# A two-layer mixture-of-experts and attention kernel: earlier index compaction, outputs on ScalarE, gathers issued ahead of scatters

## The chip, the cores and the metric

One core of a Trainium2 chip runs the whole program. The metric is the device time of one execution in microseconds. Before the change three runs gave 1326.40, 1332.17 and 1331.73 us, median 1331.73.

## The reference

For x of 4 batches, 1024 tokens and 128 features, all in float32:

```
x = x + 0.5 * ffn(layernorm(x))
x = x + attention(layernorm(x))     # 16 heads of 8, 3D rotary positions
x = x + 0.5 * ffn(layernorm(x))     # same weights
```

In ffn eight experts each choose the 256 tokens of a batch with the highest affinity (a softmax over experts), and

```
x_in = x[bidx, idx]                          # gather, 256 rows per batch and expert
h = silu(x_in @ w_gate.T) * (x_in @ w_up.T)  # 128 -> 512
x_e = h @ w_down.T                           # 512 -> 128
out = zeros.at[bidx, idx].add(gating * x_e)  # scatter-add
```

## The kernel before, in words

There are three stages: experts, attention, experts. Each expert stage works through 16 passes, 0 to 15 and 16 to 31: first the eight experts for batches 0 and 1, then the eight for batches 2 and 3. Pass `it` (function `expert` of each engine) handles 512 rows, 256 of each of two batches. All engines have an instruction order of their own, written out by hand, and meet only at semaphores, each of which is named `s_...`.

**The way of one expert j.** DVE (VectorE) builds a one-hot matrix of 128 x 256 for each of 16 token blocks (`onehots`, L1362, in quarters of four). TensorE multiplies it by a table with five columns for each token: two parts of the row number, three parts of the gating factor (`compact`, L1041, 32 small matmuls). DVE reads the result from PSUM (`pick`, L1369 to L1377): row numbers `idx`, factors `gain`. POOL (GpSimd) issues four indirect DMAs, 128 rows each, that gather the tokens (`gather`, L535). TensorE transposes them (`turn_tokens`, L1051), ScalarE copies them out of PSUM (L784). Then come the gate and up projections in four slices (`gate_up`, L1061 and L1062), silu on ScalarE (L793), the product on DVE (`hidden`, L1394), the down projection (`down`, L1072), scaling by `gain` out of PSUM (`outputs`, L1385, on DVE), and four indirect DMAs that add the rows in DRAM (`scatter`, L553).

**How the passes overlap.** In pass `it` TensorE computes gate and up of expert `it` in slices 0 to 3. Behind slice 1 it computes the down projection of expert `it - 1` and then compacts expert `it + 2`; behind slice 2 it transposes the tokens of expert `it + 1`. DVE calls `outputs(it - 1)` and then `pick(it + 2)` behind the second product. POOL calls `scatter(it - 1)` and then `gather(it + 2)`. SP loads the weights of expert j after the down projection of expert j - 2.

**Waits around the change.** A gather waits for its indices and for the transposes of expert j - 2. A scatter waits for its outputs and until the scatter before it, into the same rows' tensor, has landed. `pick(j)` writes buffer j % 4 and, at L1369 to L1371, waits until the scatter of expert j - 4, which reads its indices there, has landed:

```
                if j >= 4:
                    for b in batches(j - 4):
                        dve.wait_ge(s_scat[b], adds_before(j - 4) + 32)
```

`hidden(it, u)` waits for silu; `gate_up(it + 1, 0)` on TensorE waits for `hidden(it, 2)`. In front of slot tables (`all_onehots`) `expert_values` copies the slots and factors of one expert into `slotE` and `valsE`.

**What stands between.** The table of `tables()` puts other work at places (it, k), done by `between`: in passes 0 to 5 and 16 to 22 the search for the routing thresholds of the next half ("f": a scan of 1024 affinities on DVE, L1275, then a small matmul, ten rounds), in passes 10 to 15 the attention's projections ("s": a matmul into one bank of PSUM, which DVE or ScalarE must read before the next). For the attention each rotated projection is split into three bfloat16 parts: `high` and `middle` on ScalarE, `rest` (L580) and `lowest` (L584) on POOL. The factors of the next half are split in three by `gains` on POOL (L566 to L576). After scatter 6 and 7, and after 14 and 15, SP reloads X (`load_x`), of which DVE takes the moments in pass 9 and in the attention. SP then stores the parts and loads the groups for the attention (`store_parts`, `load`). The attention starts on TensorE when the outputs of expert 15 are written.

## Time and profile before

| | us |
|---|---|
| median of three runs | 1331.73 |
| profiled execution | 1333.52 |
| its span, first to last instruction | 1331.7 |
| DVE busy | 1044.5 |
| TensorE busy (matmul) | 1122.5 |
| ScalarE busy | 768.2 |
| POOL busy | 448.9 |
| mean granted TensorE clock | 0.944 of 2.4 GHz |

Busy times are sums over the whole span; the stages have different limits, so a share says little of a single one. In the profile a line such as L1072 is a line of the kernel, "x32" counts instructions merged in the row, and what stands behind "<-" is what ended the idle time in front of it. POOL's rows for indirect DMAs are the time of issuing them; the data lands later. Names of tiles are those of the memory: `xt`, `ye`, `sg` and `hid` all lie in `Pt`.

### The profile page before, as it was taken

What the parts mean: (1) busy time and instruction counts of PE and PEld (TensorE: products, weight loads), DVE (VectorE), ACT (ScalarE), POOL (GpSimd) and SP (SyncE); (2) the same over time, 40 slices, a digit from 0 to 9 for tenths busy, and PEclk for the clock granted to TensorE, in tenths of its full rate; (3) what the DMA queues carried; (4) which work ended last, traced back from release to release, by engine and by line L of the source; (5) the groups of instructions that cost most, each with busy time, mean ns of one, the idle gap of its engine ahead of it and who ended that gap; (6) DMA issues with size and microseconds to landing.
All of it is one profiled execution on the core that took longest, in us unless ns stands there. A gap on an engine that the chain in (4) does not pass through costs nothing.

```text
span 1331.7 us, 25142 instructions
## 1 busy us (share of the span) xinstructions
PE 1122.5 (84%) x9424; PEld 476.4 (36%) x9424; DVE 1044.5 (78%) x2182; ACT 768.2 (58%) x1433; POOL 448.9 (34%) x431
## 2 busy tenths in 40 slices
PE   3159898999487999999899998899978889889884
PEld 3126565666131222222222222122313256556553
DVE  3676966764986999999999999899896685975531
ACT  2043112532246999999789996889778843121120
POOL 3034777688256111100000000004000025777674
PEclk9999999999587999999999998999999988999887
DMA  8023446456612311112201131101220224444442
GB/s 264 6 56 68 82 86 141 82 128 139 174 43 80 87 31 38 43 43 52 63 17 31 41 82 48 40 8 41 73 57 4 56 58 95 100 87 85 104 89 20
DMA packets 92122, 94.54 MB, mean 71 GB/s; under 512 B 14464, under 2 KB 68992, under 8 KB 91968
## 3 DMA queue, kind: packets, MB, share of 16 engines
q1 hardware_dynamic: 69472, 76.13, 20.5%
q0 software_dynamic: 22528, 16.79, 9.6%
q8 instruction: 75, 1.23, 0.4%
q14 instruction: 47, 0.39, 0.1%
HBM read 63.12 MB, written 31.59 MB: 71 GB/s over the span
## 4 chain that ended last, share of the span: by engine, by line
DVE 50%; PE 25%; POOL 8%; issue 7%; ACT 5%; DMA 3%; DVEq 0%; POOLq 0%; ACTq 0%
DVE mx L1549 34%; PE pA L1072 4%; PE pS L1061 4%; DVE ge L1275 4%; POOL out_dram L553 3%; PE pO L1185 3%; PE pO L1062 2%; DMA xg<-zd,idx 2%; DVE onehot L1362 2%; POOL x L553 2%; ACT Pt L893 2%; DVE scr L1434 2%; PE pS L1206 2%; POOL xg L535 2%; PE pS L1062 1%
## 5 line engine op out<-in xcount | busy, mean ns | idle before, releaser
L1549 DVE TENSOR_REDUCE mx<-pA 128x2 f32<-128x1024 f32 x512 | 589.3, 1216 | 26.8 <-PE pA L1117 25.3
L893 ACT ACTIVATE Pt<-pS 128x512 f32<-128x512 f32 x1024 | 556.2, 596 | 75.7 <-PE pS L1206 70.3
L1185 PE MATMUL pO<-Pt,Vst 128*16 128x256 f32 x4096 | 327.9, 393 | 11.5 <-ACT U L884 11.5
L793 ACT ACTIVATE Pt<-pS 128x512 f32<-128x512 f32 x128 | 76.3, 597 | 245.6 <-PE pS L1061 245.4
L595 POOL TENSOR_TENSOR mparts<-mx,onesm 128x32 bf16<-128x32 f32 x16 | 4.0, 252 | 518.0 <-DVE mx L1554 511.3
L1117 PE MATMUL pA<-Kst,Qst 48*128 48x512 bf16 x704 | 144.3, 406 | 36.6 <-DVE mx L1549 34.8
L535 POOL DMA_INDIRECT xg<-zd,idx x128 | 125.7, 982 | 142.0 <-issue 73.1
L1061 PE MATMUL pS<-Pt,wg 128*128 128x512 f32 x256 | 147.6, 660 | 14.5 <-DVE Pt L1394 9.4
L1206 PE MATMUL pS<-Qst,Kst 51*128 51x512 bf16 x704 | 141.5, 398 | 10.7 <-ACT Pt L893 5.1
L1185 PEld LDWEIGHTS pO<-Pt,Vst 128*16 128x16 f32 x4096 | 68.3, 94 | 206.5 <-issue 116.7
L1072 PEld LDWEIGHTS pA<-wd,Pt 128*128 128x128 f32 x1024 | 120.9, 192 | 20.3 <-issue 15.0
L1072 PE MATMUL pA<-wd,Pt 128*128 128x128 f32 x1024 | 122.3, 276 | 2.2 <-DVE Pt L1394 2.2
L553 POOL DMA_INDIRECT x<-Pt,idx x64 | 101.0, 1578 | 58.2 <-issue 29.0
L1362 DVE TENSOR_SCALAR onehot<-slots,slotE 128x256 bf16<-128x256 bf16 x512 | 115.9, 305 | 1.4
L1206 PEld LDWEIGHTS pS<-Qst,Kst 51*128 51x128 bf16 x704 | 34.5, 93 | 166.4 <-ACT Pt L893 147.6
L1394 DVE TENSOR_TENSOR Pt<-Pt,pO 128x512 f32<-128x512 f32 x64 | 43.9, 686 | 62.3 <-PE pO L1062 47.0
L1385 DVE TENSOR_SCALAR Pt<-pA,gain 128x128 f32<-128x128 f32 x128 | 36.0, 344 | 60.2 <-PE pA L1072 56.1
L1062 PE MATMUL pO<-Pt,wu 128*128 128x512 f32 x128 | 71.1, 639 | 0.0
L1062 PE MATMUL pS<-Pt,wu 128*128 128x512 f32 x128 | 69.1, 623 | 0.0
L1117 PE MATMUL pA<-pair 48*128 48x512 bf16 x320 | 62.8, 388 | 5.8 <-DVE mx L1549 5.8
L1394 DVE TENSOR_TENSOR Pt<-Pt,pS 128x512 f32<-128x512 f32 x64 | 43.8, 685 | 29.5 <-ACT Pt L793 14.3
L784 ACT ACTIVATE Pt<-pA 128x512 f32<-128x512 f32 x32 | 19.1, 596 | 81.9 <-PE pA L1051 81.9
(170 smaller groups left out, 1140.0 us busy)
## 6 DMA issues: line engine op xcount, KB each, us to landing
wg<-w_gate_dram SPq DMA_DIRECT2D x32, 256.0 KB, 2.8
wu<-w_up_dram SPq DMA_DIRECT2D x32, 256.0 KB, 3.1
wd<-w_down_dram SPq DMA_DIRECT2D x32, 256.0 KB, 3.9
qk<-parts SPq DMA_DIRECT2D x64, 96.0 KB, 2.7
Kst<-qk SPq DMA_DIRECT2D x132, 32.0 KB
zd<-Z SPq DMA_DIRECT2D x8, 512.0 KB, 4.1
vp<-pair SPq DMA_DIRECT2D x4, 1024.0 KB, 5.3
Vst<-vp SPq DMA_DIRECT2D x16, 256.0 KB
```

Source lines behind the costliest of these rows:

```text
L535: pool.indirect_dma_start(xg[p][:, k, :], None, zd[j // E % 2], bass.IndirectOffsetOnAxis(idx[j % 4][:, k:k + 1], 0)).then_inc(s_gath[p], 16)
L553: pool.indirect_dma_start(acc, bass.IndirectOffsetOnAxis(rows[j % 4][:, k:k + 1], 0), ye[j % 2][:, k, :], None, compute_op=ALU.add).then_i ...
L893: S.activation(Pt[:, s % 4, j, r * 512:(r + 1) * 512], pS[:, bank_of(k, 4 * s + 2 * j + r), :], ACT.Exp, scale=SCALE).then_inc(s_exp, 1)
L1061: M.matmul(pG[u % 2], wg[p][:, u * P:(u + 1) * P], xt[:, p, :], start=True, stop=True).then_inc(s_gate, 1)
L1062: M.matmul(pU[u % 2], wu[p][:, u * P:(u + 1) * P], xt[:, p, :], start=True, stop=True).then_inc(s_up, 1)
L1072: last = M.matmul(pY[:, k * D:(k + 1) * D], hid[p][:, i, k * P:(k + 1) * P], wd[p][:, i, :], start=(i == 0), stop=(i == IC - 1))
L1117: last = M.matmul(pA[ring[q, a] % 2][:, r, :], Qst[k][64 * r:64 * r + 48, j, c * P:(c + 1) * P], Kst[k][64 * r:64 * r + 48, j, half * 512: ...
L1185: last = M.matmul(pO[32 * h:32 * h + 16, cols], Vst[k][:, s % 8, h, :], Pt[:, s % 4, h // 2, (h % 2) * 512 + 256 * a:(h % 2) * 512 + 256 * ...
L1206: last = M.matmul(pS[:, bank_of(k, n + r), :], Kst[k][64 * r:64 * r + ROWS, j, (s % 8) * P:(s % 8 + 1) * P], Qst[k][64 * r:64 * r + ROWS, ...
L1362: last = V.tensor_scalar(onehot[:, b, c, :], slots[:, :], slotE[:, c * HB + b:c * HB + b + 1], None, ALU.is_equal)
L1394: V.tensor_tensor(hid[it % 2][:, u, :], sg[:, u % 2, :], pU[u % 2], ALU.mult).then_inc(s_hid, 1)
L1549: V.reduce_max(mx2[:, k, 2 * j:2 * j + 2, c, half], pA[ring[q, a] % 2][:, :, :], AX.X).then_inc(s_Ar, 1)
```

## The change

TensorE compacts expert `it + 2` right behind gate and up slice 1, ahead of the down projection. DVE picks behind the second product, ahead of `between(it, 1)`; it sums the parts straight out of PSUM, with one conversion to integers behind it. `expert_values` goes: one-hots and compaction read `slotT` and `vals` in place. `outputs` runs on ScalarE, behind `between(it, 1)`, with the factor as the activation's scale. POOL issues `gather(it + 2)` ahead of `scatter(it - 1)`, except in pass 22. `rest` and `lowest` of tiles 0 and 1 run on DVE in passes 12 to 14; those of tiles 2 and 3 stay on POOL, behind `scatter(15)`, and ScalarE's `middle(2)` moves behind pass 15. On SP `load(0)`, `load(1)` and `store_values(1)` come ahead of the weights of expert 16, and `store_parts(2)` comes behind the reload of X.

```diff
@@ SP
+            load(0)
+            load(1)
+            store_values(1)
             load_weights(16)
-            load(0)
             load_weights(17)
-            store_parts(2)
-            store_values(1)
             for b in range(2, B):
                 sp.wait_ge(s_scat[b], 256)
                 load_x(b, x1_in)
+            store_parts(2)
             store_parts(3)
-            load(1)
@@ POOL
             for it in range(RUN):
-                if 13 <= it:
-                    lowest(it - 13)
-                if it in (12, 13):
-                    rest(it - 12)
+                if it + 2 < RUN:
+                    gather(it + 2)
                 if it:
                     scatter(it - 1)
-                if it + 2 < RUN:
-                    gather(it + 2)
                 if it == 2:
                     gains(1)
-                if it in (14, 15):
-                    rest(it - 12)
             scatter(RUN - 1)
+            rest(2)
+            rest(3)
+            lowest(2)
             lowest(3)
...
             for it in range(RUN, NIT):
+                if it + 2 < NIT and it != 22:
+                    gather(it + 2)
                 if it > RUN:
                     scatter(it - 1)
-                if it + 2 < NIT:
+                if it == 22:
                     gather(it + 2)
@@ ScalarE
+            def outputs(j):
+                act.wait_ge(s_down, j + 1)
+                act.wait_ge(s_idx, j + 1)
+                if j >= 2:
+                    for b in batches(j - 2):
+                        act.wait_ge(s_scat[b], adds_before(j - 2) + 32)
+                for k in range(HB * SH):
+                    last = S.activation(ye[j % 2][:, k, :], pY[:, k * D:(k + 1) * D], ACT.Copy, scale=gain[j % 4][:, k:k + 1])
+                last.then_inc(s_ye, 1)
...
                         between(it, 1)
+                        if it % RUN:
+                            outputs(it - 1)
                         between(it, 2)
@@ TensorE
                 gate_up(it, 1)
+                if it % RUN < RUN - 2 and it != 22:
+                    compact(it + 2)
                 if not first:
                     down(it - 1, (0, 1))
                 between(it, 1)
                 if not first:
                     down(it - 1, (2, 3))
-                if it % RUN < RUN - 2 and it != 22:
-                    compact(it + 2)
@@ DVE, pick
-                link(V.tensor_copy(picked[r][:, :, :], pI[:, 0:5 * HB * SH].rearrange("p (k f) -> p k f", f=5)))
-                V.tensor_tensor(idx[r][:, :], picked[r][:, :, 0], picked[r][:, :, 1], ALU.add).then_inc(s_idx, 1)
+                picked = pI[:, 0:5 * HB * SH].rearrange("p (k f) -> p k f", f=5)
+                V.reduce_sum(gain[r][:, :], picked[:, :, 2:5], AX.X)
+                V.reduce_sum(row[:, :], picked[:, :, 0:2], AX.X).then_inc(s_row, 1)
+                dve.wait_ge(s_row, j + 1)
+                V.tensor_copy(idx[r][:, :], row[:, :]).then_inc(s_idx, 1)
...
-                link(V.tensor_tensor(gsum[:, :], picked[r][:, :, 2], picked[r][:, :, 3], ALU.add))
-                link(V.tensor_tensor(gain[r][:, :], gsum[:, :], picked[r][:, :, 4], ALU.add))
@@ DVE, expert
                 hidden(it, 1)
-                between(it, 1)
-                if not first:
-                    outputs(it - 1)
                 if it + 2 < end and it != 22:
                     pick(it + 2)
-                    if quarters:
-                        expert_values(it + 3)
-                        onehots(0)
+                between(it, 1)
+                if it + 2 < end and it != 22 and quarters:
+                    onehots(it + 3, 0)
                 between(it, 2)
```

## Rows read from the trace of the kernel before

**Rows 1.** the page, busy time of each engine

```profile
PE 1122.5 (84%) x9424; PEld 476.4 (36%) x9424; DVE 1044.5 (78%) x2182; ACT 768.2 (58%) x1433; POOL 448.9 (34%) x431
```

**Rows 2.** the page, shares of the chain that ended last, by engine

```profile
DVE 50%; PE 25%; POOL 8%; issue 7%; ACT 5%; DMA 3%; DVEq 0%; POOLq 0%; ACTq 0%
```

**Rows 3.** windows, passes 3, 12, 25, 26: length, PE, PEld, DVE, ACT, POOL busy, clock, DMA

```profile
132.00:149.00 17.00, 13.28 (x90) 8.31 (x89) 16.30 (x59) 2.99 (x5) 13.96 (x15) 0.96 0.40 78
...
266.00:281.30 15.30, 15.30 (x100) 9.97 (x99) 10.51 (x34) 5.66 (x11) 12.54 (x10) 1.00 0.45 88
...
1211.30:1223.70 12.40, 12.40 (x85) 8.16 (x84) 7.87 (x31) 2.99 (x5) 7.61 (x7) 0.95 0.43 99
1223.70:1241.50 17.80, 14.11 (x86) 8.81 (x85) 7.95 (x31) 2.99 (x5) 14.45 (x11) 0.86 0.47 84
```

**Rows 4.** timeline of TensorE in pass 24; start us, us, what, idle before

```profile
1199.69 3.73 PE L1072 MATMUL pA<-wd,Pt 128*128 128x128 f32 x32
1203.27 0.95 PE L1041 MATMUL pA<-valsE,onehot 128*128 128x5 bf16 x32
...
1208.03 0.66 PE L1051 MATMUL pA<-ident,xg 128*128 128x128 f32 x4 [1.99 <-DMA xg<-zd,idx]
```

**Rows 5.** timeline of POOL, passes 23 and 24

```profile
1185.57 1.01 POOL L535 DMA_INDIRECT xg<-zd,idx  x1 [0.30 <-issue]
...
1192.66 1.62 POOL L553 DMA_INDIRECT out_dram<-Pt,idx  x1 [2.15 <-DVE Pt L1385]
...
1200.38 1.01 POOL L535 DMA_INDIRECT xg<-zd,idx  x1 [0.31 <-issue]
...
1204.23 0.94 POOL L535 DMA_INDIRECT xg<-zd,idx  x1 [0.30 <-issue]
```

**Rows 6.** timeline of DVE in pass 24

```profile
1203.47 1.12 DVE L1385 TENSOR_SCALAR Pt<-pA,gain 128x128 f32<-128x128 f32 x4 [2.81 <-PE pA L1072]
1204.51 0.17 DVE L1372 COPY picked<-pA 128x20 f32<-128x20 f32 x1
...
1205.58 1.03 DVE L1362 TENSOR_SCALAR onehot<-slots,slotE 128x256 bf16<-128x256 bf16 x4
```

**Rows 7.** timeline of all engines, the pick of expert 16 and its gather

```profile
1060.75 0.18 DVE L1372 COPY picked<-pA 128x20 f32<-128x20 f32 x1 [3.87 <-PE pA L1041]
...
1060.96 0.17 DVE L1373 TENSOR_TENSOR idx<-picked 128x4 int32<-128x4 f32 x1
...
1061.95 1.09 POOL L535 DMA_INDIRECT xg<-zd,idx  x1 [51.65 <-DVE idx L1373]
```

**Rows 8.** chain in order of time; start us, us, what

```profile
291.46 2.21 DVE idx L1373
...
1257.43 4.37 DMA out_dram<-Pt,idxo
...
1307.75 1.55 POOL out_dram L553
...
1313.31 3.33 DMA out_dram<-Pt,idxo
1317.52 1.55 POOL out_dram L553
```

**Rows 9.** DMA issues, the last scatters; last column median us from issue to landing

```profile
out_dram<-Pt,idxo POOLq DMA_INDIRECT x32, 3.3
```

**Rows 10.** two lines of the code: durations ns min/median/max

```profile
L722 ACT ACTIVATE pair<-pA x16: 271/280/297, 268.8 to 325.5; 128x128 f32<-128x128 f32 x16
...
L580 POOL TENSOR_TENSOR scr<-scr,parts x8: 2115/2130/2719, 274.2 to 430.1; 128x1024 f32<-128x1024 f32 x8
```

**Rows 11.** timelines of DVE and POOL in passes 2 and 3

```profile
125.31 1.12 DVE L1385 TENSOR_SCALAR Pt<-pA,gain 128x128 f32<-128x128 f32 x4 [3.71 <-PE pA L1072]
...
139.69 0.47 POOL L566 TENSOR_TENSOR half<-affc,halves 128x128 f32<-128x128 f32 x1
...
143.39 1.64 POOL L553 DMA_INDIRECT x<-Pt,idx  x1 [0.31 <-issue]
```

More of the change, by code:

```diff
@@ L160, in program @@
         res = [sb(f"res{i}", [P, CH, ROWS_H], F32) for i in range(2)]
-        slotE = sb("slotE", [P, HT], F32)
-        valsE = sb("valsE", [P, HT, 5], BF16)
         onehot = sb("onehot", [P, HB, CH, CAP], BF16)
-        picked = [sb(f"picked{i}", [P, HB * SH, 5], F32) for i in range(4)]
-        gsum = sb("gsum", [P, HB * SH], F32)
+        row = sb("row", [P, HB * SH], F32)
         idx = [sb(f"idx{i}", [P, HB * SH], I32) for i in range(4)]
@@ L247, in program @@
         s_comp = sem("comp")
+        s_row = sem("row")
         s_idx = sem("idx")
@@ L815, in _ @@
                 expert(it)
+            outputs(RUN - 1)
+            middle(2)
             middle(3)
@@ L927, in _ @@
                 expert(it)
+            outputs(NIT - 1)
         @block.tensor
@@ L1036, in compact @@
                     pe.wait_ge(s_idx, j)
+                if j % E == 0:
+                    pe.wait_ge(s_vals, 6 * (j // E + 1))
                 for b in range(HB):
@@ L1460, in between @@
                     scale_and_shift(5)
+                if (it, k) == (12, 1):
+                    rest(0)
+                if (it, k) == (12, 3):
+                    lowest(0)
+                if (it, k) == (13, 2):
+                    rest(1)
+                if (it, k) == (14, 0):
+                    lowest(1)
                 if (it, k) == (16, 0):
@@ L1500, in expert @@
                 if quarters and it != 22:
-                    onehots(1)
+                    onehots(it + 3, 1)
                 between(it, 3)
@@ L1543, in _ @@
                 expert(it)
-            outputs(RUN - 1)
             def piece(q, a):
@@ L1607, in _ @@
                 expert(it)
-            outputs(NIT - 1)
 def constants():
```

44 lines of the change are left out of this document (17 added, 27 removed).

## The prediction, made before the changed kernel ran

> **What bounds the kernel now.** The page's busy times come first [rows 1]: no engine is full, and the mean hides stages with different limits. The shares of the chain [rows 2] say the same: half of it is VectorE, most of that in the attention, whose instructions the change doesn't touch. So the two expert stages count. Cut into passes, one window for each [rows 3], they show three kinds. Pass 3 has its limit on VectorE (16.3 of 17.0 us busy; passes 3, 4, 20 and 21 are like it, where the search for the routing threshold runs between the experts). Pass 12 has it on TensorE (15.30 of 15.30; passes 10 to 15 carry the attention's projections). Passes 25 and 26 alternate between 12.4 us, TensorE full, and 17.8 us, in which it is idle.
>
> Why it is idle is in the timelines. In pass 24 the transposes of the next tokens wait 1.99 us for the gather [rows 4]. POOL's own timeline says why the gather is late [rows 5]: the four scatters start at 1192.66, the four gathers of expert 25 only behind them at 1200.38. Both had been released together: the scatters wait for VectorE's outputs, and pick follows these outputs on VectorE by about a microsecond [rows 6]. A set of scatters takes 7.4 us of POOL, 0.3 us lie between, a set of gathers 4.8 us (1200.38 to 1204.23 and 0.94): 12.6 us a pass with the second gap, near TensorE's 12.4. Later in the same rows' stretch the transposes start 2.9 us after the gathers' issue ended (1205.17 to 1208.03).
>
> **The change, part by part.** I write pick(j) for the step that makes expert j's indices; it runs in pass j - 2.
>
> Gather before scatter. POOL's order becomes gather(j), scatter(j - 3), gather(j + 1), scatter(j - 2). The gathers go out as soon as pick(j) is done, and they land long before the transposes: that idle time goes. What is late next is a wait that stays as it was, in pick: before it writes the buffer j % 4, it waits until scatter(j - 4) has landed. In the old order a whole set of gathers and the next set of scatters lay between. In the new order scatter(j - 4) is the last thing on POOL before gather(j), and gather(j) waits for pick(j). So a closed lap arises, from pick to pick:
> - pick done to first gather 0.8 us (1061.13 to 1061.95 [rows 7]),
> - gathers 4.8 and a gap of 0.3 [rows 5],
> - scatters from the first issue until the last has landed: 8.9 by the chain (1307.75 to 1313.31, and 3.33 [rows 8]), 9.2 by POOL's slower set (5.9 to the last issue [rows 5], and 3.3 [rows 9]),
> - pick 0.5: the old one took about 0.4 for two dependent steps [rows 7], the new one has three.
> The lap is 15.3 to 15.6 us; I take 15.5, as the scatters that stand beside a working VectorE are the slower ones. It is longer than POOL's 12.6 and TensorE's 12.4, and about what two passes take now (12.4 and 17.8, mean 15.1 [rows 3]). VectorE stands in the wait, and behind it are the next one-hots and the third hidden product, for which TensorE's next pass waits: TensorE is idle in one piece of about 3 us a pass, a little over the 1.99 us of pass 24; TensorE's granted clock was below its full 2.4 GHz in some of the passes with such waits (mean 0.86 in pass 26 [rows 3]). That costs nothing while the lap sets the pace.
>
> Compact before down (TensorE). Nothing is added; 0.95 us [rows 4] moves ahead of the 3.7 us of the down projection. Picks come 3.7 us earlier where nothing else holds them; down, outputs, scatter and the next weights' load, which waits for down, come 0.95 later. Inside a lap both are covered: the scatter's data is there about 8 us before POOL comes to it.
>
> Outputs on ScalarE. Four activations; the nearest row, 128x128 out of PSUM, has 0.28 us each [rows 10], 1.1 in all, against 1.12 on VectorE [rows 6]. ScalarE has the room (3 us busy of 12 to 17 [rows 3]). Bounds 0.8 to 2.0 us; nobody waits for them inside a lap.
>
> Slots and factors read in place, pick by sums. From the start of the outputs to the first one-hot VectorE spent 2.1 us (1203.47 to 1205.58 [rows 6]); 0.5 stay. So 1.6 us less in each pass. It counts only in passes on VectorE's limit.
>
> Rest and lowest of two tiles go from POOL (2.13 us each [rows 10]) to VectorE; the latter has room in passes 12 to 14 (10.5 of 15.3 us busy [rows 3]). Pick(15) once took 2.21 us [rows 8] beside such a POOL operation; this is gone. The Trainium skill's page "SBUF — State Buffer" (section "SBUF: two separate sides") has a rule for this, that a VectorE operation with two inputs in SBUF and a GpSimd operation that reads SBUF shut each other out; the row agrees. The two that stay on POOL now run behind scatter(15), beside the first attention pieces; bounds 0 to +2 us, I take 0, since nobody needs their result for 20 us. SP's order: the loads of the first two attention groups come earlier, the third weights' load later, needed 700 us on; 0.
>
> **The sum, first stage.** Pick(4) is free of the loop, pick(5) nearly. The old outputs(1) began at 125.31 [rows 11]; with 0.95 for compact, 1.1 on ScalarE, 0.8 of waking and 7.5 of scatters POOL is at 135.7; the gains' three subtractions and casts take 3.7 (139.69 to 143.39), gathers and gap 5.1, scatter(2) lands 8.9 later and pick(6) follows by 0.5: 153.9. This is ahead of the old one, by what pass 3 and the early compaction save. From there nine laps of 15.5 give pick(15) at 293.4; the old one was done at 293.7 (291.46 and 2.21 [rows 8]). **The lead is used up: -0.3.** Against it: the reload of X for the attention waits for scatter(6) and (7), which are late in their lap, and VectorE then waits in pass 9; with TensorE full from pass 10 on this stays: 0 to +2, I take +1. ScalarE no longer waits for POOL in pass 15: 0 to -2, I take -0.8. Start of both stages: two copies fewer, -0.3.
>
> **Second stage.** Picks 18 to 21 wait for nothing. Passes 19 to 22 lose up to 1.6 us each of VectorE (0 to -6.4), but POOL's own chain of scatters and gathers follows close behind; I take -0.9. In pass 22 the old order stays. Gather(24) starts at 1185.57 [rows 5] less 0.9; gather(25) 5.1 later, scatter(22) 5.1 later, landed after 9, pick(26) at 1204.5, against 1204.9 before. Five laps: pick(31) at 1282.0. Then 0.8, 5.1, and three more scatter sets of 8.9 with 0.9 of waking each (1316.64 to 1317.52 [rows 8]) until the last one starts, at 1317.3. It was 1317.52: -0.2.
>
> Sum: -0.3 + 1.0 - 0.8 - 0.3 - 0.2 = -0.6 us. The profiled execution took 1333.5 us (span 1331.7), 1.8 above the median of the runs; on the median this is **1331.1 us**.
>
> **The rivals.** A (0.50): as above, between 1325 and 1338.
> B (0.21): the lap is shorter, and what the early gathers free is kept. The lap's largest piece is the landing, 3.3 of 15.5 us; where it counts less, each lap gains until POOL's 12.6. With a lap of 14.35 nine laps outside TensorE's passes gain 1.15 each and five inside 0.2 (15.3 is TensorE's): -11 us, 1320. With no wait at all 9 x 2.9 + 1 = 27 us: 1304. For it: POOL has nothing else to do. Against it: 3.3 and 3.33 agree in two views. The Trainium skill's page "DMA: Bandwidth & Descriptors" (section on the anatomy of one DMA) fits such a DMA with 2.0 us and the bytes over 436 GB/s; for 64 KB this makes 2.15 us, and the lap would be the 14.35 of this rival; the rows here speak for 3.3.
> C (0.24): slower. The same lap, with landings that are late under the weights' loads, which now fall into it. The chain has one scatter with 4.37 [rows 8]. If that is the rule, a lap has 16.6 us, and 14 laps cost +15: 1346. It decides from a lap of 15.95 on (14 x 0.48 = 6.7 us). For it: VectorE and with it all engines now stand in every lap, nothing is left to absorb a late one.
> D (0.05): the scatter order doesn't matter in either direction, nothing moves: 1331.7.
>
> **How the numbers follow.** 0.5% (6.7 us) is about what a measurement of this kernel can tell from no change. Of A 0.40 lie within, 0.05 on either side. B: 0.19 faster, 0.02 within. C: 0.22 slower, 0.02 within. D: within. So faster 0.24, same 0.49, slower 0.27. The range of 8 in 10 takes A, the better part of B and C up to its price: 1316 to 1345. A's own is 1325 to 1338.
>
> **What would show it.** Right: VectorE idle before the new pick's first sum, released by the scatters' DMA, in passes 4 to 13 and 24 to 29, some 2 to 4 us each; passes there of an even 15.5 us; no wait of the transposes for a gather; POOL idle about 3 us a pass before the gathers, none before the scatters. Passes 3 and 20 shorter by 1 to 2 us. Wrong: passes 24 to 30 below 14.5 us (B), above 16 (C), or a wait of POOL before the scatters, which would mean that ScalarE's outputs are late and the lap isn't what I hold it to be.

## The result and the profile after

The changed kernel took 1355.56 us (median of four runs, 1353.56 to 1355.91); the kernel before 1330.16 beside it. The ratio is 1.019, 95% interval 1.016 to 1.022: slower by 25 us in the medians. Forecast were 1331.1 us and no difference; the result lies above the range.

The page, busy times and the shares of the chain, against [rows 1, 2]:

```profile
PE 1130.3 (83%) x9424; PEld 477.3 (35%) x9424; DVE 998.1 (74%) x1962; ACT 802.8 (59%) x1561; POOL 440.8 (33%) x427
...
DVE 42%; PE 20%; POOL 9%; issue 6%; DMA 5%; ACT 4%; SPq 0%; POOLq 0%; DVEq 0%; ACTq 0%
```

VectorE lost 46 us of work, as intended, and ScalarE gained 35; TensorE's 8 more are the same matmuls at a lower granted clock. What grew in the chain is DMA, from 3% to 5%: work went down and waiting went up.

Cut into passes (windows as in [rows 3]; passes 3, 9, 10, 12, and 25 to 27):

```profile
128.97:147.58 18.61, 15.49 (x88) 10.85 (x89) 14.48 (x52) 4.02 (x9) 13.05 (x15) 0.82 0.35 70
219.85:241.83 21.98, 13.73 (x84) 8.32 (x85) 11.00 (x59) 5.61 (x12) 14.56 (x13) 0.83 0.50 120
241.83:260.14 18.31, 17.03 (x100) 10.56 (x101) 7.50 (x32) 12.87 (x30) 12.50 (x11) 0.83 0.41 76
275.35:290.64 15.29, 15.29 (x100) 9.68 (x98) 10.86 (x29) 6.58 (x15) 10.03 (x9) 1.00 0.43 87
1223.35:1237.68 14.33, 12.04 (x85) 7.75 (x85) 5.38 (x22) 4.02 (x9) 8.43 (x7) 1.00 0.45 87
1237.68:1254.61 16.93, 13.71 (x85) 8.29 (x85) 6.44 (x26) 4.02 (x9) 10.24 (x9) 0.90 0.37 78
1254.61:1271.69 17.08, 13.71 (x85) 8.31 (x85) 6.18 (x26) 4.02 (x9) 10.23 (x9) 0.90 0.38 78
```

The even passes that were forecast for 24 to 29 are there from 26 on, but they have 17 us and not 15.5, and no engine is busy for more than 13.7 of them. Pass 3 has grown from 17.0 to 18.6 while VectorE's work in it fell from 16.3 to 14.5.

The sum over the profiled executions, from the start of each pass (its first gate product) to that of the next, in us:

| stretch | before | after | difference |
|---|---|---|---|
| start to pass 2 | 115.7 | 113.7 | -2.1 |
| passes 2 to 5 | 61.7 | 63.8 | +2.1 |
| passes 6 to 8 | 42.1 | 42.3 | +0.3 |
| **passes 9 and 10** | 31.3 | 40.3 | **+9.0** |
| passes 11 to 14 | 61.1 | 61.1 | +0.1 |
| **pass 15 and the attention** | 758.2 | 760.8 | **+2.6** |
| **passes 16 to 23** | 126.1 | 128.8 | **+2.7** |
| **passes 24 to 30** | 102.4 | 108.4 | **+6.0** |
| pass 31 to the last landing | 27.8 | 29.8 | +2.0 |

That is +22.6 us; the spans differ by 22.4. The first line isn't the change's: it is 115.7 and 115.8 in two later runs of the changed kernel. These are single executions; a second one of the kernel before (e9) has 95.2 in passes 24 to 30. The bold stretches and the passes in front of them follow one by one.

**Passes 24 to 30: the lap.** All engines' timeline, a lap and a half of it (compare [rows 4 to 6]):

```profile
1247.75 1.57 POOL L551 DMA_INDIRECT out_dram<-Pt,idxo  x1 [0.30 <-issue]
1252.57 0.17 DVE L1380 TENSOR_REDUCE gain<-pA 128x4 f32<-128x12 f32 x1 [8.73 <-DMA out_dram<-Pt,idxo]
1252.85 0.17 DVE L1383 CAST idx<-row 128x4 int32<-128x4 f32 x1
1253.88 1.01 POOL L533 DMA_INDIRECT xg<-zd,idx  x1 [4.56 <-DVE idx L1383]
1254.61 1.81 PE L1073 MATMUL pS<-Pt,wg 128*128 128x512 f32 x2 [3.22 <-DVE Pt L1393]
1259.00 1.62 POOL L551 DMA_INDIRECT out_dram<-Pt,idxo  x1 [0.30 <-issue]
1260.62 3.82 PE L1084 MATMUL pA<-wd,Pt 128*128 128x128 f32 x32
1264.47 0.33 SPq L346 DMA_DIRECT2D wg<-w_gate_dram  x1
1264.68 1.55 POOL L551 DMA_INDIRECT out_dram<-Pt,idxo  x1 [0.30 <-issue]
1265.33 0.43 SPq L348 DMA_DIRECT2D wd<-w_down_dram  x1
1269.65 0.17 DVE L1380 TENSOR_REDUCE gain<-pA 128x4 f32<-128x12 f32 x1 [8.88 <-DMA out_dram<-Pt,idxo]
```

The lap is as described: pick waits for the landing of scatter(j - 4); the gathers follow pick by 0.9 us, the scatters follow the gathers by 0.3, nothing waits for outputs, and the transposes wait for no gather. TensorE stands 3.2 us for the product behind pick on VectorE. But the lap has 17.08 us (1252.57 to 1269.65). Its one odd piece stands in the chain, in order of time, the last scatters of sets 24 to 27:

```profile
1247.75 4.70 DMA out_dram<-Pt,idxo
...
1264.68 4.85 DMA out_dram<-Pt,idxo
...
1281.74 4.74 DMA out_dram<-Pt,idxo
...
1298.76 5.02 DMA out_dram<-Pt,idxo
```

In [rows 8] the last one had 3.33. The forecast's lap of 15.5 and 1.4 to 1.7 us more for the landing make 16.9 to 17.2. What coincides with it stands between the rows of the timeline: SP loads the next weights, three times 256 KB, as soon as the down projection is done (1260.62 and 3.82 give 1264.44; SP issues at 1264.47), and the last scatter is issued at 1264.68. In all four of these laps the first load goes out 0.2 to 0.3 us ahead of the last scatter. In the first stage the lap is closed too, but shorter: from gather 6 (155.49) to gather 15 (298.23) nine laps have 15.9 us in the mean, and the last scatters of sets 8 to 11 land after 3.2 to 3.3. The view of DMA issues doesn't show the late landings, since its last column is a median over all 32:

```profile
out_dram<-Pt,idxo POOLq DMA_INDIRECT x32, 3.3
```

**The cost of the wait on the page.** Two groups, busy and mean ns, then the idle time ahead of them. The 163.8 us hold one wait of 52 us behind the attention that the kernel before has as well [rows 7]; the 35.5 us are the four laps of the second stage behind scatters 24 to 27, and all waits of pick for scatters together have 75.5 us.

```profile
L533 POOL DMA_INDIRECT xg<-zd,idx x128 | 124.9, 976 | 233.4 <-DVE idx L1383 163.8
...
L1380 DVE TENSOR_REDUCE gain<-pA 128x4 f32<-128x12 f32 x32 | 5.4, 170 | 83.8 <-DMA out_dram<-Pt,idxo 35.5
```

**Passes 9 and 10: scatter 7.** Timeline of all engines in pass 9:

```profile
230.04 1.56 POOL L551 DMA_INDIRECT x<-Pt,idx  x1 [0.31 <-issue]
234.38 0.17 DVE L1380 TENSOR_REDUCE gain<-pA 128x4 f32<-128x12 f32 x1 [8.36 <-DMA x<-Pt,idx]
...
235.51 1.64 DVE L1273 BATCH_NORM_STATS2 stats<-X 128x6 f32<-128x128 f32 x8
...
238.56 1.64 DVE L1273 BATCH_NORM_STATS2 stats<-X 128x6 f32<-128x128 f32 x8 [0.53 <-DMA X<-x]
...
241.83 2.05 PE L1073 MATMUL pS<-Pt,wg 128*128 128x512 f32 x2 [8.24 <-DVE Pt L1393]
```

VectorE stands in pick(11) until scatter 7 has landed. Only then come the moments of the reloaded X, 5.5 us of work (235.51 to 241.0), and only behind these the hidden product that TensorE needs: 8.2 us idle. Scatter 7 started at 224.29, against 216.00 before. From pass 11 on TensorE is full, as in [rows 3], and the delay stays to the end of the stage.

**Passes 3 and 20: compact ahead of down.** Timeline of pass 20, where the threshold search runs on VectorE:

```profile
1155.96 0.59 PE L1053 MATMUL pA<-vals,onehot 128*128 128x5 bf16 x16 [2.55 <-DVE onehot L1368]
...
1156.41 3.40 PE L1084 MATMUL pA<-wd,Pt 128*128 128x128 f32 x16
...
1159.85 0.16 DVE L1320 TENSOR_SCALAR step<-pA 128x1 int32<-128x1 f32 x1 [2.82 <-PE pA L978]
```

TensorE waits 2.6 us in compact for one-hots that the busy VectorE has not written. The down projection, ready to run, stands behind it; half of it then takes 3.40 us at a lower clock (0.58 granted in these 3.40 us; the other half 2.03); and VectorE in its turn waits 2.8 us for the search's small matmul behind both.

**Pass 17: late weights.** It has grown from 16.4 to 18.4 us. The gate product of pass 18, after and before:

```profile
1113.89 1.10 PE L1073 MATMUL pS<-Pt,wg 128*128 128x512 f32 x2 [2.94 <-DMA wd<-w_down_dram]
```

```profile
1100.69 1.10 PE L1061 MATMUL pS<-Pt,wg 128*128 128x512 f32 x2 [1.47 <-DMA wd<-w_down_dram]
```

SP loads the weights of expert 18 behind the down projection of expert 16, and this projection now stands behind compact: the first load goes out 11.6 us after the start of the pass (10.3 before), and TensorE waits 1.5 us longer for the weights. No lap covers it here.

**The attention's start: VectorE shut out.** Timeline behind the last scatter of the first stage:

```profile
346.72 1.55 POOL L551 DMA_INDIRECT x<-Pt,idx  x1 [6.64 <-DMA x<-Pt,idx]
...
357.45 4.78 POOL L582 TENSOR_TENSOR parts<-scr,parts 128x1024 bf16<-128x1024 f32 x2
...
359.67 2.59 DVE L1278 TENSOR_SCALAR veps<-mv 128x8 f32<-128x8 f32 x1
```

Scatter 15 waits 6.6 us for scatter 14, whose last part lands 5.8 us after its issue ended (2.2 before), with SP's loads of the first attention groups and of weights beside it. This has only moved, though: in the kernel before it was scatter 15 whose last part landed 5.8 us after its issue ended, and counted from the start of pass 15 its last part lands after 34.9 us there and 35.1 here. What is new is VectorE: it sets the pace here, and has 2.59 us in an operation that takes 0.17 elsewhere, beside POOL's rest and lowest, which the change put behind scatter 15. It ends at 362.26, POOL's two operations at 362.23.

### The profile page after: what moved, and what is told of

Same layout as the page of the kernel before. It is cut to its first block, busy times and chain, and to the rows that moved or that the text cites. A ratio compares the mean times of both kernels' runs of the same rounds, so it can differ in the third digit from the quotient of the medians.

```text
span 1354.1 us, 25041 instructions
## 1 busy us (share of the span) xinstructions
PE 1130.3 (83%) x9424; PEld 477.3 (35%) x9424; DVE 998.1 (74%) x1962; ACT 802.8 (59%) x1561; POOL 440.8 (33%) x427
## 4 chain that ended last, share of the span: by engine, by line
DVE 42%; PE 20%; POOL 9%; issue 6%; DMA 5%; ACT 4%; SPq 0%; POOLq 0%; DVEq 0%; ACTq 0%
DVE mx L1558 34%; POOL out_dram L551 4%; PE pA L1084 4%; POOL xg L533 3%; PE pS L1073 3%; PE pO L1197 3%; DMA out_dram<-Pt,idxo 2%; ACT Pt L902 2%; DVE scr L1441 2%; PE pS L1218 2%; DVE ge L1287 2%; PE pS L1074 2%; PE pA L1129 1%; POOL x L551 1%; PE pO L1074 1%
## 5 line engine op out<-in xcount | busy, mean ns | idle before, releaser
L1558 DVE TENSOR_REDUCE mx<-pA 128x2 f32<-128x1024 f32 x512 | 589.2, 1216 | 34.0 <-PE pA L1129 32.2
L533 POOL DMA_INDIRECT xg<-zd,idx x128 | 124.9, 976 | 233.4 <-DVE idx L1383 163.8
L1084 PE MATMUL pA<-wd,Pt 128*128 128x128 f32 x1024 | 128.5, 283 | 2.2 <-DVE Pt L1393 2.2
L789 ACT ACTIVATE Pt<-pA,gain 128x128 f32<-128x128 f32 x128 | 36.6, 368 | 147.9 <-PE pA L1084 143.1
L551 POOL DMA_INDIRECT x<-Pt,idx x64 | 102.6, 1603 | 41.4 <-issue 18.6
L1368 DVE TENSOR_SCALAR onehot<-slots,slotT 128x256 bf16<-128x256 bf16 x512 | 112.6, 299 | 0.6
L1073 PEld LDWEIGHTS pS<-Pt,wg 128*128 128x128 f32 x256 | 44.9, 206 | 88.4 <-issue 78.3
L1074 PE MATMUL pS<-Pt,wu 128*128 128x512 f32 x128 | 75.9, 679 | 0.0
L1129 PE MATMUL pA<-pair 48*128 48x512 bf16 x320 | 62.7, 388 | 5.9 <-DVE mx L1558 5.9
L1380 DVE TENSOR_REDUCE gain<-pA 128x4 f32<-128x12 f32 x32 | 5.4, 170 | 83.8 <-DMA out_dram<-Pt,idxo 35.5
```

Source lines behind the costliest of these rows:

```text
L533: pool.indirect_dma_start(xg[p][:, k, :], None, zd[j // E % 2], bass.IndirectOffsetOnAxis(idx[j % 4][:, k:k + 1], 0)).then_inc(s_gath[p], 16)
L551: pool.indirect_dma_start(acc, bass.IndirectOffsetOnAxis(rows[j % 4][:, k:k + 1], 0), ye[j % 2][:, k, :], None, compute_op=ALU.add).then_i ...
L1073: M.matmul(pG[u % 2], wg[p][:, u * P:(u + 1) * P], xt[:, p, :], start=True, stop=True).then_inc(s_gate, 1)
L1074: M.matmul(pU[u % 2], wu[p][:, u * P:(u + 1) * P], xt[:, p, :], start=True, stop=True).then_inc(s_up, 1)
L1084: last = M.matmul(pY[:, k * D:(k + 1) * D], hid[p][:, i, k * P:(k + 1) * P], wd[p][:, i, :], start=(i == 0), stop=(i == IC - 1))
L1129: last = M.matmul(pA[ring[q, a] % 2][:, r, :], Qst[k][64 * r:64 * r + 48, j, c * P:(c + 1) * P], Kst[k][64 * r:64 * r + 48, j, half * 512: ...
```

## The experiments

Fifteen runs on four chips; e5 and e13 are the changed kernel again, e9 the kernel before. On two of the chips the kernel before takes 1348 to 1350 us, on the other two 1328 to 1330, so only ratios compare across chips. The passes are sums from the profiled executions, in us, as in the table above.

| run | us | ratio [95%] | 2-5 | 9, 10 | start of 15 | 15 to 16 | 16-23 | 24-30 |
|---|---|---|---|---|---|---|---|---|
| before | 1330.2 | 1 | 61.7 | 31.3 | 311.9 | 758.2 | 126.1 | 102.4 |
| changed | 1355.6 | 1.019 [1.016, 1.022] | 63.8 | 40.3 | 321.3 | 760.8 | 128.8 | 108.4 |
| *chip A, before 1348.4* | | | | | | | | |
| e1 | 1339.7 | 0.992 [0.990, 0.995] | 66.0 | 31.5 | 315.8 | 762.6 | 135.5 | 92.8 |
| e2 | 1359.8 | 1.007 [1.004, 1.010] | 64.6 | 34.6 | 322.0 | 762.2 | 134.2 | 101.8 |
| e3 | 1371.0 | 1.016 [1.013, 1.019] | 65.4 | 38.8 | 334.5 | 762.5 | 130.5 | 107.4 |
| e4 | 1355.6 | 1.005 [1.003, 1.007] | 62.0 | 39.0 | 320.5 | 761.3 | 136.5 | 99.1 |
| *chip B, before 1349.6* | | | | | | | | |
| e5 changed | 1360.8 | 1.008 [1.005, 1.010] | 64.3 | 38.9 | 321.2 | 762.0 | 136.9 | 101.8 |
| e6 | 1366.4 | 1.012 [1.010, 1.015] | 64.9 | 39.7 | 328.6 | 762.5 | 131.8 | 106.9 |
| e7 | 1359.9 | 1.008 [1.005, 1.010] | 63.9 | 37.2 | 319.4 | 760.0 | 136.8 | 104.4 |
| e8 | 1316.5 | 0.976 [0.974, 0.979] | 56.5 | 38.2 | 307.3 | 759.3 | 127.1 | 83.8 |
| *chip C, before 1328.2* | | | | | | | | |
| e9 before | 1327.5 | 1.000 [0.998, 1.002] | 62.9 | 31.0 | 314.9 | 758.3 | 125.2 | 95.2 |
| e10 | 1348.2 | 1.016 [1.013, 1.019] | 62.7 | 34.2 | 316.9 | 761.0 | 127.1 | 102.7 |
| e11 | 1312.4 | 0.988 [0.985, 0.991] | 56.1 | 37.4 | 305.9 | 757.6 | 124.8 | 82.1 |
| e12 | 1317.5 | 0.992 [0.990, 0.995] | 63.0 | 34.7 | 312.1 | 756.0 | 125.1 | 81.5 |
| *chip D, before 1329.9* | | | | | | | | |
| e13 changed | 1352.8 | 1.017 [1.014, 1.019] | 63.3 | 39.9 | 322.9 | 760.8 | 127.1 | 109.2 |
| e14 | 1352.3 | 1.018 [1.016, 1.020] | 64.3 | 38.1 | 319.0 | 759.2 | 124.4 | 106.6 |
| e15 | 1326.1 | 0.997 [0.996, 0.999] | 62.4 | 38.1 | 314.8 | 763.2 | 128.7 | 81.8 |

**e1: eight buffers, so that pick waits for scatter(j - 8).** `idxo` and `gain` likewise.

```diff
-        idx = [sb(f"idx{i}", [P, HB * SH], I32) for i in range(4)]
+        idx = [sb(f"idx{i}", [P, HB * SH], I32) for i in range(8)]
 ...
             def pick(j):
-                r = j % 4
+                r = j % 8
                 dve.wait_ge(s_comp, j + 1)
-                if j >= 4:
-                    for b in batches(j - 4):
-                        dve.wait_ge(s_scat[b], adds_before(j - 4) + 32)
+                if j >= 8:
+                    for b in batches(j - 8):
+                        dve.wait_ge(s_scat[b], adds_before(j - 8) + 32)
```

> The changed kernel with eight buffers for indices and gains in place of four, so that pick(j) no longer waits for scatter(j - 4); the order gather before scatter stays. Theory (the closed lap pick, gather, scatter, landing, pick sets the pace): the lap opens, passes 24 to 30 fall from 16.9 us to 12.4 to 13.5 (POOL's 12.6 or TensorE's 12.4), passes 6 to 9 too; in all 30 to 45 us less than the changed kernel: 1312 to 1325 us, below the kernel before. Rival (ScalarE's outputs and the compaction ahead of down are what costs): the wait goes but the time stays above 1345.

Windows of passes 26 and 27:

```profile
1242.43:1255.19 12.76, 12.01 (x85) 7.72 (x85) 6.33 (x25) 4.02 (x9) 9.76 (x8) 1.00 0.52 103
1255.19:1267.95 12.76, 12.01 (x85) 7.72 (x85) 6.84 (x26) 4.02 (x9) 10.32 (x9) 1.00 0.53 105
```

12.8 in place of 17 us, at full clock, since pick no longer waits for a scatter. Passes 9 and 10 are back at 31.5 us too. The change with this edit beats the kernel before: the lap is the largest single cause, in both stages. The gain is smaller than expected, though: 1339.7 us lies above the 1312 to 1325, and it is 16 us less than the first result of the changed kernel and 21 less than e5, on a chip of the same speed, not 30 to 45. Passes 2 to 5 and 16 to 23 (66.0 and 135.5 us) stay close to e5's 64.3 and 136.9, without the ring.

**e2: POOL's order back, scatters first, the rest of the change kept.**

```diff
+                if it:
+                    scatter(it - 1)
                 if it + 2 < RUN:
                     gather(it + 2)
-                if it:
-                    scatter(it - 1)
 ...
-                if it + 2 < NIT and it != 22:
-                    gather(it + 2)
                 if it > RUN:
                     scatter(it - 1)
-                if it == 22:
+                if it + 2 < NIT:
                     gather(it + 2)
```

> The changed kernel with POOL's order alone put back: scatter(it - 1), then gather(it + 2). Theory: pick(j) again has a set of gathers and one of scatters between it and the scatter it waits for, no wait in pick; time at or a little below the kernel before, 1320 to 1332. Rival: if the other parts cost, it stays above 1340.

**e3: the kernel before with the order of POOL turned, and nothing else.** The reverse of the diff above.

> The kernel before with POOL's order alone changed (gather ahead of scatter). Theory: the swap by itself closes the lap, whatever else is changed: pick waits for the scatters' landing, laps of 16 to 17.5 us, 1350 to 1362 us. Rival (the early compaction is needed for the loss, as it makes pick arrive early): the pick comes late in the pass anyway and the time is within 5 us of the kernel before.

Windows: of e2 passes 26 and 27, then of e3 pass 26:

```profile
1247.79:1264.31 16.52, 13.32 (x85) 8.23 (x86) 5.97 (x24) 4.02 (x9) 13.02 (x11) 0.92 0.49 87
1264.31:1277.65 13.34, 12.55 (x85) 7.88 (x84) 7.21 (x26) 4.01 (x9) 7.41 (x7) 0.97 0.40 93
```

```profile
1255.03:1271.91 16.88, 13.70 (x84) 8.39 (x85) 7.96 (x33) 2.98 (x5) 10.37 (x9) 0.90 0.38 78
```

e2 alternates again as [rows 3] do, e3 has the even lap of 16.9. The turned order alone closes the lap; the earlier compaction and the cheaper pick don't open it. e2 is still slower than before by 0.7%: the old order doesn't win back what the rest of the change costs, as its rival said. And the parts don't add: the turned order alone costs 1.6%, the rest alone 0.7%, both together 0.8% on the next chip (e5), where the kernel before is as fast as here.

**e4: gate and up weights loaded ahead of the down projection, only the third load behind it.**

```diff
                 if j >= 2:
-                    sp.wait_ge(s_down, j - 1)
+                    sp.wait_ge(s_gate, 4 * (j - 1))
+                    sp.wait_ge(s_up, 4 * (j - 1))
                 ...
+                if j >= 2:
+                    sp.wait_ge(s_down, j - 1)
                 sp.dma_start(wd[p][:, :, :], t["w_down"][e].rearrange("(i p) d -> p i d", p=P)).then_inc(s_w[p], 16)
```

> The changed kernel with the loads of w_gate and w_up issued as soon as the up projection of expert j - 2 is done, and only w_down behind its down projection. Theory (in the lap the weights' loads fall on the last scatter's landing each time and stretch it from 1.7 to 3.3 us): landings fall to about 2.3 us, laps of passes 24 to 30 from 16.9 to about 16, time 8 to 14 us below the changed kernel: 1342 to 1348. Rival (landings are long for another reason, the scatters themselves or the rows they add to): laps stay at 16.9, time within 3 us of the changed kernel.

The chain, the last scatters of three laps:

```profile
1238.19 3.37 DMA out_dram<-Pt,idx
...
1253.86 3.31 DMA out_dram<-Pt,idxo
...
1269.47 3.34 DMA out_dram<-Pt,idxo
```

With two of the three loads moved 12 us away from the last scatter, the landing is back at the 3.3 of [rows 8, 9], and the picks of experts 27 to 31 follow each other by 15.6 to 15.8 us: the lap of the prediction. It isn't short enough to help: e4 is still 0.5% slower than the kernel before, and at 1355.6 us above the 1342 to 1348 expected. The collision is worth 1.4 us a lap, the lap itself the rest.

**e5: the changed kernel once more.**

> The changed kernel once more, beside the others on one chip, as their base. It gave a ratio of 1.019 to the kernel before on the first chip; nothing in any theory ties that to the chip, so 1.016 to 1.022 here. Laps of 16.5 to 17.3 us in passes 25 to 29, as before. If the lap were only just closed, a chip with slightly faster landings would give well under 1.015.

The change costs 0.8% there, not 1.9, outside the 1.016 to 1.022 expected. Most of the difference is in the kernel before, which took 1.5% more on this chip, the changed one 0.4%.

**e6: compact and pick at their old places in the search passes.**

```diff
+SEARCH = (2, 3, 4, 5, 18, 19, 20, 21)
 ...
-                if it % RUN < RUN - 2 and it != 22:
+                if it % RUN < RUN - 2 and it != 22 and it not in SEARCH:
                     compact(it + 2)
 ...
+                if it in SEARCH:
+                    compact(it + 2)
 ...
-                if it + 2 < end and it != 22:
+                if it + 2 < end and it != 22 and it not in SEARCH:
                     pick(it + 2)
                 between(it, 1)
+                if it in SEARCH:
+                    pick(it + 2)
```

> The change, with compact and pick at their old places (behind the down projection and behind VectorE's pieces between) in passes 2 to 5 and 18 to 21 alone. Theory H (compact ahead of down is a head-of-line block on TensorE where VectorE is late with the one-hots): passes 3 and 20 fall from 18.6 and 17.8 us to about 17; the start of pass 24 counted from that of pass 16 falls from 128.8 to 126 or 127 us; the whole is 2 to 5 us shorter than the changed kernel, ratio to the kernel before about 1.016. In the first stage little comes through, since the lap closed over the scatters takes over from pass 7. Rival R (the passes are long since the new pick and the new rest and lowest on VectorE fall there, wherever compact stands on TensorE): nothing moves, 1.019.

Neither theory. Pass 3 took 18.0 us (16.5 in e5), pass 20 17.9 (19.0). Passes 16 to 23 fell by 5 us against e5, as H says, but the first stage got 7 us longer and passes 24 to 30 5 us: scatters 3 to 6 landed 2.9 to 3.1 us behind the end of their issue, in e5 scatters 3 to 5 in 1.6 to 1.7. That the later picks bring the lap into the bad phase early fits these landings, but no run tests it.

**e7: SP's order back.** `load(0)` behind the weights of expert 16, `store_values(1)` behind those of 17, `load(1)` behind the stores of the parts.

> The change, with SP's three loads of the attention's first groups put back behind the weights of experts 16 and 17 as in the kernel before. Theory S: these loads run beside the landing of scatter 14 (5.8 us) and hold scatter 15 back, which holds the reload of X and with it the attention: the start of pass 16 comes 2 to 3.5 us earlier against the end of the first stage, the whole is as much shorter, ratio about 1.0165. Rival P (what is late in the attention's start is VectorE, shut out by the rest and lowest on POOL, which now stand behind scatter 15): nothing moves, 1.019, and VectorE's 128x8 operation beside them still takes 2.6 us in place of 0.17.

The whole didn't move. The stretch from pass 15 to pass 16 is 2.0 us shorter than in e5, scatter 14 lands in 2.4 us in place of 5.5, and VectorE's small operation has 0.17 us: with scatter 15 earlier, it no longer fell beside POOL's (these end at 356.91, the operation starts at 357.74). Counted from the start of pass 15, scatter 15 lands after 32.2 us, 34.5 in e5.

**e8: e1, e4, e6 and e7 together.**

> The change with four things on top: eight buffers for the indices in place of four, gate and up weights loaded ahead of the down projection, compact and pick of the search passes and SP's three loads at their old places. If the lap is the main cost and the other three are small and apart, the ring takes 1.019 to 0.992 as on the first chip, search and SP's order take 0.003 to 0.006 more, the early weights nothing (they only shortened the lap that the ring removes): 0.986 to 0.990. If the early weights also relieve the landings that other steps wait for, or the costs add in full, 0.975 to 0.983. Above 0.992 would mean that at least one of the three is a loss without the lap.

0.976, the far end of what was expected: the three edits that gave little or nothing inside the lap (e6 a loss) give 1.6% on top of the ring, against e1's 0.992 on a chip of the same speed. Passes 2 to 5 are at 56.5 us, against 64 to 66 in e1 and e5. Passes 9 and 10 stay long (38.2 us) though no pick waits for a scatter any more: VectorE now waits 4.3 and 2.1 us for the reloaded X itself.

**e9: the kernel before once more.**

> The kernel before, for its profile on this chip: on the two chips since the first it took 1348 to 1350 us, 18 more than on the first, while the changed kernel took only 5 more on one of them. If the chip is slower throughout (clock, DMA), all three stages are longer by about 1.4%: the attention by 10 us, the expert stages by 3 us each. If it is the loop ye, scatter, gather, transposes of passes 23 to 30 that falls into a worse alternation, the attention is 4 us longer, as in all runs there (762 against 758), and passes 16 to 31 carry 10 us or more.

The chip was not one of the two that take 1348, so the question stayed open. What it shows: a second profiled execution of the same kernel has 95 us in passes 24 to 30, not 102. Windows of passes 25 and 26:

```profile
1213.02:1225.44 12.42, 11.98 (x86) 7.81 (x85) 7.86 (x31) 2.98 (x5) 9.33 (x8) 1.00 0.51 106
1225.44:1239.52 14.08, 11.98 (x86) 7.80 (x84) 8.16 (x31) 2.98 (x5) 11.34 (x10) 1.00 0.50 97
```

The alternation of 12.4 and 17.8 in [rows 3] was one draw; these two passes have a mean of 13.3. The prediction's "what two passes take now, mean 15.1" leaned on a single execution.

**e10: the change, with scatter 7 ahead of gather 10 in pass 8.**

```diff
-                if it + 2 < RUN:
+                if it + 2 < RUN and it != 8:
                     gather(it + 2)
                 if it:
                     scatter(it - 1)
+                if it == 8:
+                    gather(it + 2)
```

> The change, with POOL's order turned back in pass 8 of the first stage alone: scatter 7 ahead of gather 10, as before. Theory X: what stretches passes 9 and 10 (22.0 and 18.3 us against 16.4 and 14.9) is that scatter 7 lands late there, with pick 11, the reload of X and its moments behind it on VectorE; scatter 7 comes 7 to 8 us earlier, passes 9 and 10 fall to about 17 and 16 us, the end of the first stage comes 5 to 8 us earlier and the whole is as much shorter: 0.994 to 0.996 of the changed kernel, 1.002 to 1.005 of the kernel before on the last chip's scale. Rival Y (the closed lap sets the end of the first stage anyway, whatever pass 9 does): the stage ends within 2 us of where it did, no change.

Scatter 7 starts at 218.4 (226.2 in e13), passes 9 and 10 have 34.2 us (39.9), the stage ends 6.0 us earlier: X, in the traces. In the medians 1348.2 against 1355.6 and 1352.8 of the changed kernel on chips of the same speed; the intervals of the ratios overlap, so for the whole it is likely, not shown.

**e11: e8 with the same edit.**

> The four-part version of the last call (0.976) with scatter 7 ahead of gather 10 as well. There is no lap in it, but VectorE waits 4.3 and 2.1 us for the reload of X in pass 9 and TensorE stands 8.4 us. X: scatter 7 starts some 5 us earlier and the whole is 4 to 6 us shorter, 0.972. Y: gather 10 is late in its place and nothing is won, 0.976.

Nearer to Y. Scatter 7 came only 2.5 us earlier, since it now waited for scatter 6 to land, and gather 10 came 10 us later (215.9 against 205.8), with TensorE waiting for it. Passes 9 and 10 have 37.4 us against 38.2. With 1312.4 us it is the shortest time of all, 1.2% below the kernel before on that chip.

**e12: e11 with compact ahead of down in the search passes as well.**

> As the run above, but with compact ahead of the down projection in the search passes too, as the change has it. Theory H (there TensorE stands in compact for one-hots of a VectorE that is busy with the search): passes 16 to 23 take 5 to 8 us more than in the run above (they took 135.5 us with the ring alone, 127.1 in the four-part version), passes 2 to 5 one to 3 more: 0.977 to 0.980. Rival R (with the lap gone it makes no difference where compact stands): 0.972.

H holds in the first stage: passes 2 to 5 take 63.0 us against 56.1, and the stage ends 6.2 later. In the second the 4.8 us lost in passes 19 to 21 come back in passes 22 and 23, and 16 to 23 are equal (125.1 and 124.8), where 5 to 8 us were expected. The medians are 5 us apart; the intervals of the two ratios overlap a little.

**e13: the changed kernel on the fourth chip.**

> The changed kernel again, as the base of the next two. On a chip where the kernel before takes 1328 to 1331 us: 1355 us, ratio 1.019, passes 24 to 30 of 108 us together. On one where it takes 1348 to 1350: 1360, ratio 1.008. Anything between would say that the ratio hangs on more than the chip.

The first result again, 109 us in passes 24 to 30.

**e14: rest and lowest of tiles 2 and 3 back inside the stage.**

```diff
                 if it == 2:
                     gains(1)
+                if it in (14, 15):
+                    rest(it - 12)
+            lowest(2)
             scatter(RUN - 1)
-            rest(2)
-            rest(3)
-            lowest(2)
             lowest(3)
```

ScalarE's `middle(2)` goes back into pass 15 with them.

> The change, with rest and lowest of tiles 2 and 3 back on POOL inside the last two passes of the first stage (one lowest before scatter 15, one behind it), and ScalarE's middle of tile 2 back in pass 15. Theory P (POOL's four operations behind scatter 15 shut VectorE out at the attention's start, its 128x8 operation took 2.59 us for 0.17): from the first gate product of pass 15 to that of pass 16 it is 1.5 to 3 us shorter than in the changed kernel beside it (760.8 there), the whole as much: 0.998 to 0.999 of it. Rival S (scatter 14's landing of 5.8 us and the late reload hold the start): no difference within 0.5 us. A loss is possible too, by up to 2 us, if scatter 15 then waits for POOL.

The chain at the attention's start has VectorE's operation twice:

```profile
357.46 0.17 DVE veps L1279
...
361.02 0.17 DVE veps L1279
```

Scatter 14 still lands in 6.2 us and scatter 15 when it did (35.3 us after the start of pass 15, 35.4 in e13), so S is out as the cause of what is won; the stretch is 1.6 us shorter than in e13. P holds in the trace; in the median it drowns (1352.3 and 1352.8).

**e15: the kernel before with the turned order, the eight buffers and the early weights alone.**

> The kernel before with three edits alone: gathers ahead of scatters, eight buffers for the indices, gate and up weights ahead of the down projection. If compact ahead of down, ScalarE's outputs and the reads in place are worth nothing once no lap is closed, this gives what the versions with them gave: 0.988 to 0.992 of the kernel before on a chip where that takes 1330 us. If the order of the gathers is the one part that pays, less than 0.988, since the search passes keep their old order. If the later pick (3.7 us later in each pass, behind the down projection) makes the gathers late again, above 0.995 with a wait of the transposes for the gather in passes 24 to 30.

Passes 24 to 30 are as short as in e12 (81.8 and 81.5 us), at TensorE's limit:

```profile
1218.52:1230.29 11.77, 11.77 (x85) 7.88 (x84) 8.13 (x31) 2.99 (x5) 9.34 (x8) 1.00 0.54 107
```

So there the other parts of the change add nothing, and no gather is late. The whole gains 0.3%, though, less than the 0.8 to 1.2% expected, where e12 gains 0.8 and e11 1.2. The difference to e12 is 7.2 us from pass 15 to pass 16 (763.2 against 756.0), 3.6 in passes 16 to 23 and 2.7 ahead of pass 15. Of the 7.2, 4.1 are there when the attention's first maximum (`mx`) is done: 26.7 us after the start of pass 15, in e12 22.6. Which of the parts left out gives that isn't separated.

## Why the prediction was wrong

**Right:** the closed lap, its place, its order of pieces, who waits behind it, that the transposes' wait goes and that POOL idles ahead of the gathers. ScalarE's outputs take 1.14 us for a set, forecast 1.1, and in the laps nobody waits for them. The work saved on VectorE is saved. Pick 6 comes at 154.6, forecast 153.9. The 0.8 us at the end of the first stage are won: the attention's first maximum is done 22.6 us after the start of pass 15, 23.3 before. e3 shows that the lap comes from the turned order alone, e4 shows it at 15.6 us.

**Where the time went,** forecast and measured between the profiled executions: to the start of pass 15 +0.4 and +9.4 us, from there to pass 16 -0.8 and +2.6, from pass 16 on -0.2 and +10.7. Two terms make most of it, the lap's size in the second stage and the reload of X in the first.

**Wrong, the lap's size.** The step that failed is the third piece of the lap, "scatters from the first issue until the last has landed: 8.9 by the chain ... 9.2 by POOL's slower set". The landing of 3.3 us was read where nothing stood beside it. Inside the lap of the second stage it is 4.7 to 5.0, beside the same three weights' loads in four laps running, and 3.3 again in e4, where two of the three are moved away. This was rival C, with its mechanism and nearly its price for a lap there (16.6, measured 17.0), at 0.24 against 0.50 for A. C had the sum wrong too: its 1346 takes 16.6 in all 14 laps, and the nine of the first stage have 15.9. The wrong thought was that a late landing is an accident, once in a while, as the single 4.37 in [rows 8] seemed to say. In a closed lap what the lap releases nearly keeps its phase, so a late landing comes back: sets 24 to 27 here, 25 to 27 in e5. It isn't strict: in e14 set 25 lands after 3.4 us between late ones. VectorE's wait in such a lap, given as 2 to 4 us among the signs, is 8.7 to 9.1. The prediction never set the loads beside the scatters. In this trace, counted from the end of pick (1253.02), the gate product starts at 1.6 us, the down projection is done and the loads go out at 11.4, the last scatter is issued at 11.7. And "about what two passes take now, mean 15.1" set the lap beside one slow draw; e9 has 13.3. The Trainium skill's page "DMA: Bandwidth & Descriptors" (section on latency and other measured facts) has the latency of HBM rise from 0.2 to 2 us at high load; the traces agree in direction, with 1.4 us between the landings of e4 and those of the changed kernel. The fit of one DMA on the same page of the Trainium skill, which gave rival B its 14.35, has 2.15 us where e4 still measures 3.3.

**Wrong, "the reload of X ... 0 to +2, I take +1".** It was +9.0 in passes 9 and 10, the largest single miss. The prediction's own laps put pick(10) at 215.9 and so scatter 7 at 221.8, 5.8 us later than before (216.00); I set the result beside pick(15) alone, which was equal, and didn't carry the delay of scatter 7 into the pass that waits for it. Measured, it came 8.3 us later. The moments' 5.5 us then stand behind pick's wait instead of beside it, and e10, with scatter 7 alone ahead of its gather, has 5.7 us less in these two passes than e13. In all seventeen traces pass 11 starts 34.2 to 36.9 us after scatter 7 does, with a lap and without one. From pass 11 on TensorE is full and pick(15) doesn't decide: it came 3.7 us later, the stage 9.4.

**Wrong, compact before down: "Nothing is added".** True of work, not of order: in the search passes it puts a wait on VectorE ahead of work that was ready. "Passes 3 and 20 shorter by 1 to 2 us" became 1.6 and 1.7 longer (20: 16.15 to 17.82). Without the lap this is worth 6 us in the first stage (e11, e12). And the next weights' load that comes 0.95 later, "inside a lap" covered, isn't covered in pass 17, where no lap is closed: TensorE waits 1.5 us more for it.

**Wrong, the +0 of rest and lowest on POOL.** The prediction had such a rule, for operations with two inputs, and the place, bounds 0 to +2, and took 0 with "since nobody needs their result for 20 us". The cost isn't that of the result; it is of the neighbour who is shut out, and that was VectorE, the bound of the stage: 2.59 us for 0.17. Measured 1.6 (e14). The Trainium skill's page "SBUF — State Buffer" (section "Who interferes with whom") names VectorE's tensor_scalar among the operations that can take the shared port; the trace agrees, with this 128x8 one, which ends with POOL's.

**Left open.** Why the kernel before takes 1.4 to 1.5% more on two of the chips, and with it why the ratio is 1.008 on one and 1.017 to 1.019 on others; there is no trace of it there. Passes 16 to 23 of the changed kernel, 128.8 and 127.1 us on the first chip and on D, but 136.9 on chip B, belong to the same question. The traces say where these 9.8 us (e5 against e13) are, not why: 5.0 in pass 23, at whose end TensorE waits 5.0 us for expert 24's weights (4.7 to 5.8 in e1, e4 and e7 as well, no such wait in e13), and 3.5 in pass 18, in which TensorE is busy almost throughout at a granted clock of 0.73 in the mean, in e13 0.83. How much of e7's 2.0 us is scatter 15's earlier landing and how much VectorE's operation isn't separated.

## What to carry to other kernels

Turning a queue's order can close a loop through a buffer's reuse; then what is in the loop nearly keeps its phase against the other transfers, and a collision can be paid turn after turn. Lay all transfers of one turn on one time axis before pricing it, and try the deeper ring first: eight buffers of a few bytes took the change from 0.8 to 1.9% slower to 0.8% faster than the kernel before. An early step placed ahead of ready work on an engine that keeps its order is only free where its input is never late. And carry each delayed event to all that wait for it, the rare waits (a reload, a stage's end) too.

## What was not expected of the hardware

In the trace of the changed kernel a scatter's last part lands 3.2 to 3.3 us after its issue begins in sets 8 to 11, with no weights' load near it. It took 4.7 to 5.0 us in sets 24 to 27, where three loads of 256 KB are issued from 0.3 us before to 1.1 behind its start, and 3.9 us in set 28, with the loads 1.9 to 0.6 us ahead. In the view of medians all of these are the same 3.3. An operation of VectorE with one input of 128x8 floats took 2.23 to 3.18 us in eight traces beside POOL's 128x1024 operations, ending 0.04 us behind the last of them each time, and 0.17 in e7, e11, e14 and e15, where it stood clear of them. In the lap TensorE's granted clock was 0.90 in the mean, with 3.2 us of idle time a pass, and 1.00 in the passes of 12.8 us without it.
